# Cross-attention, mixture of experts and self-attention on one core: two hand-written step lists for the first and the steady walk, and the second batch's keys loaded apart from its values

## The reference

```python
x = x + xattn(layernorm(x), ctx)      # softmax((q Wq + bq)(ctx Wk + bk) / 8) (ctx Wv + bv) Wo + bo
z = layernorm(x)
h = z + rmsnorm(causal_attention(z) @ wo)
dense = h + rmsnorm(silu(h @ w1) * (h @ w3) @ w2)
sparse = rmsnorm(sum over the top 2 experts of prob * expert(z))
out = x + dense + sparse
```

## Time and profile before

| | us |
|---|---|
| three runs | 1542.5, 1551.01, 1550.32 |
| median | 1550.32 |
| the profiled execution | 1540.53 (span of its instructions 1538.8) |
| PE busy | 1357.7 (88%) |
| PE weight loads busy | 844.2 |
| DVE, ACT, POOL busy | 812.8, 572.5, 591.5 |
| granted TensorE clock, mean | 0.966 of 2.4 GHz |

### The profile page before, as it was taken

The page is one execution under the profiler, slowest core; times in us unless marked ns, Lnnn a source line. Parts: engine busy times, 40 slices in busy tenths (PEclk is TensorE's granted clock), DMA queues, the critical chain, the costliest instruction groups (busy, mean ns, idle before and its releaser), DMA issues. The chain is left out here.

```text
span 1538.8 us, 21916 instructions
## 1 busy us (share of the span) xinstructions
PE 1357.7 (88%) x6989; PEld 844.2 (55%) x6990; DVE 812.8 (53%) x1656; ACT 572.5 (37%) x1207; POOL 591.5 (38%) x1040
## 2 busy tenths in 40 slices
PE   6997759997999898989979997989899879999995
PEld 5443425663566366646745663566366536666664
DVE  2442554476447626853774486348536823333348
ACT  2334325402630452155125403531452253443446
POOL 4111224324432534254234324331634155555544
PEclk9998969998999999999999999999999999999998
DMA  6128530350043007100700340052005434332245
GB/s 206 48 97 255 202 98 1 92 142 15 1 125 110 15 1 198 43 8 28 206 16 1 110 125 15 1 157 77 15 4 144 128 100 127 127 99 86 89 169 200
DMA packets 82264, 141.61 MB, mean 92 GB/s; under 512 B 10632, under 2 KB 66336, under 8 KB 78720
## 3 DMA queue, kind: packets, MB, share of 16 engines
q1 hardware_dynamic: 62512, 94.37, 20.2%
q10 hardware_dynamic: 13184, 28.34, 6.3%
q0 software_dynamic: 6480, 17.77, 3.4%
HBM read 84.90 MB, written 55.15 MB: 91 GB/s over the span
## 5 line engine op out<-in xcount | busy, mean ns | idle before, releaser
L1325 ACT ACTIVATE room<-ps 128x512 f32<-128x512 f32 x320 | 180.5, 598 | 175.7 <-PE ps L1061 175.0
L1648 DVE TENSOR_REDUCE nm<-ps 128x2 f32<-128x256 f32 (+3 forms) x256 | 200.2, 819 | 82.2 <-PE ps L1035 80.5
L1116 PE MATMUL ps<-hT,w 128*128 128x512 f32 x768 | 207.5, 414 | 0.0
L731 POOL TENSOR_SCALAR_AFFINE_SELECT room<-room 128x256 f32<-128x256 f32 (+1 forms) x320 | 119.8, 384 | 148.7 <-ACT room L1325 146.2
L1116 PEld LDWEIGHTS ps<-hT,w 128*128 128x128 f32 x768 | 141.5, 192 | 34.0 <-DVE hT L1678 2.0
L1034 PE MATMUL ps<-room 96*128 96x128 bf16 (+3 forms) x512 | 125.0, 312 | 32.1 <-DMA room<-parts_d 16.0
L965 PE MATMUL ps<-room,xnT 128*128 128x512 f32 x256 | 131.9, 640 | 20.7 <-ACT xnT L1211 14.5
L1061 PE MATMUL ps<-room 99*128 99x384 bf16 (+3 forms) x512 | 113.0, 310 | 29.5 <-ACT room L1325 26.9
L1152 PE MATMUL ps<-room 128*128 x284 | 135.4, 599 | 1.9 <-ACT room L1375 1.9
L1347 ACT ACTIVATE room<-ps 128x512 f32<-128x512 f32 x64 | 37.2, 592 | 267.5 <-PE ps L1116 267.5
L1126 PE MATMUL ps<-w,room 128*128 128x256 f32 x512 | 129.4, 392 | 8.1 <-DVE room L1699 8.1
(11 more groups left out here) (245 smaller groups left out, 2265.4 us busy)
## 6 DMA issues: line engine op xcount, KB each, us to landing
room<-parts_d SPq DMA_DIRECT2D x48, 256.0 KB, 9.8
room<-parts_d ACTq DMA_DIRECT2D x48, 256.0 KB, 7.4
room<-xs_d SPq DMA_DIRECT2D x71, 129.0 KB, 2.1
parts_d<-room SPq DMA_DIRECT2D x64, 128.0 KB, 1.8
vw_d<-stage ACTq DMA_DIRECT2D x8, 1024.0 KB, 4.4
room<-pair_d SPq DMA_DIRECT2D x8, 1024.0 KB, 8.0
m_d<-stage ACTq DMA_DIRECT2D x8, 896.0 KB, 5.6
room<-m_d SPq DMA_DIRECT2D x7, 1024.0 KB, 5.1
```

What stands on the lines that cost most here:

```text
L731: done(g.affine_select(out=w, in_=w, compare_op=ALU.is_ge, fill=0.0, base=0, pattern=[[0, 2]] * (blocks - 1) + [[1, P]], channel_multiplie ...
L1116: last = mm(bank(up_banks(b, m)[i]), w[:, x, k, m * P:(m + 1) * P], hT[:, y, k, :], start=((x, y, k) == terms[0]), stop=((x, y, k) == term ...
L1325: done(fn(prob[:, u * 512:(u + 1) * 512], bank(score_bank(b) + n % 2), ACT.Exp), "b_exp")
L1648: done(v.tensor_reduce(nm[:, t, 2 * hp:2 * hp + 2], pair_ps, AX.X, ALU.max, negate=True), "a_max")
```

## The change

The dealing functions go, and two lists written out by hand stand in their place, `FIRST_WALK` and `STEPS`, with the same steps as before in them (162 and 205). Counted on the lists:

- In the steady list the part up to `norm_3` is ordered anew. From there to the end it is as it was but for one step: `f_wo_sq` stands behind `qk.0` and `qk.1`, where it stood ahead of them.
- In the first walk nearly everything has another place. The last three `vw_out` stand at the very end, behind `vf.7.1`.
- `kv_in` is split: keys (`m_d`, `bqk_d`) count on it, values (`vw_d`) on a new semaphore `vw_in`. In the first walk SP issues the keys of batch 1 ahead of `send_shifts`; the values stay behind all writes of `vw_d`.
- Of the value folds DVE now copies bank 5, ACT only bank 4; and the projections `vp` go to banks 6 and 7 in turn.
- The copies that turn `wq` and `wk` stand on DVE in step `ct.2.0` of the first walk, not in `qk.0`.

```diff
-STEPS = interleaved() + TAIL
+STEPS = dealt("""
+    x_turn.0 x_turn.1 cs.0.0 f_hb sc.0.0 sc.0.1 cs.0.1 sc.0.2 sc.0.3 sc.0.4 shift.1 sc.0.5 cs.1.0 sc.0.6 sc.0.7 exp.0 va.0.0 sc.0.8 sc.0.9 sum.0
...
+    cv.2.0 cv.2.1 out_t.2 ct.3.0 ct.3.1 va.3.1 va.3.2 cv.3.0 out_t.3 cv.3.1 norm_3 f_o_turn x2_turn.0 f_wo.0 x2_turn.1 f_wo.1 qk.0 qk.1 f_wo_sq
+    f_o_norm qk.2 qk.3 v.0 v.1 f_h_turn v.2 v.3 route.0 fu.0.0 f_yb fg.0.0 fu.0.1 fg.0.1 route.1 fu.1.0 fg.1.0 fu.1.1 fg.1.1 route.2 fd.0.0 fd.0.1
...
+FIRST_WALK = dealt("""
+    x_stats x_apply kp.0 m.0 m.1 kp.1 x_turn.0 x_bias m.2 kf.0.0 x_turn.1 m.3 kf.0.1 cs.0.0 bqk.0 bqk.1 kf.1.0 cs.0.1 kp.2 vw.0 kf.1.1 exp.0 vw.1
...
+    max.6.1 max.6.2 max.6.3 vf.7.0 nx_apply max.7.0 max.7.1 vf.7.1 max.7.2 vw_out.5 vw_out.6 max.7.3 vw_out.7 shift_parts.1 z w_split
...
-            def load_kv(n):
+            def load_keys(n):
                 need(sp, n - 1, "sc_ps", T)
                 need(sp, n - 1, "sc_add", T)
-                need(sp, n - 1, "pv_ps", T)
...
+            def load_values(n):
+                need(sp, n - 1, "pv_ps", T)
...
-                    send_shifts(b, 0)
                     if c is None:
                         for i in range(2):
                             sp.wait_ge(m_out[i], 16 * KD * PAIRS // 4)
                         sp.wait_ge(p0["bqk_out"], 16)
+                        sp.sem_inc(freed, 1)
+                        load_keys(b + 1)
+                    send_shifts(b, 0)
+                    if c is None:
                         for i in range(4):
                             sp.wait_ge(kv_out[i], 16 * PAIRS // 4)
                         sp.sem_inc(freed, 1)
-                        load_kv(b + 1)
+                        load_values(b + 1)
...
-                        for j in range(2):
-                            last = fn(vw_stage[pa % 4][:, half * 2:half * 2 + 2, j * D:(j + 1) * D], bank(4 + j).rearrange("p (c m) -> p c m", m=D), ACT.Copy)
-                        last.then_inc(p0["fold_act"], 1)
+                        fn(vw_stage[pa % 4][:, half * 2:half * 2 + 2, 0:D], bank(4).rearrange("p (c m) -> p c m", m=D), ACT.Copy).then_inc(p0["fold_act"], 1)
...
+                    elif kind == "vf":
+                        pa, half = step[1:]
+                        dve.wait_ge(p0["fold_ps"], 2 * PAIRS + 2 * pa + half + 1)
...
+                        v.tensor_copy(vw_stage[pa % 4][:, half * 2:half * 2 + 2, D:], bank(5).rearrange("p (c m) -> p c m", m=D)).then_inc(p0["fold_dve"], 1)
```

More of the change, by code:

```diff
@@ L51 @@
 PER = dict(
-    x_in=16, kv_in=64, stats=4, stats1=1, mv1=1, rstd1=1, xn1=1, xT1=2, xnT=2, bq=1,
+    x_in=16, kv_in=32, stats=4, stats1=1, mv1=1, rstd1=1, xn1=1, xT1=2, xnT=2, vw_in=32,
     m_ps=10, m_act=8, m_dve=2,
@@ L98, in interleaved @@
-def interleaved():
-    first, last = CROSS.index(("cs", 0, 1)), CROSS.index(("ct", 3, 1))
-    slots = [i for i, s in enumerate(CROSS) if s[0] in ON_PE and first <= i <= last]
-    order, given = [], 0
-    for i, s in enumerate(CROSS):
-        order.append(s)
-        if i in slots:
-            want = (slots.index(i) + 1) * len(SCORES) // len(slots)
-            order += SCORES[given:want]
-            given = want
-    return order
-TAIL = [
[4 rows of a table removed]
-]
-_max = [("max", hp, t) for hp in range(H // 2) for t in range(T)]
@@ L140, in first_walk, with dealt @@
-def first_walk():
-    order = [("x_stats",), ("x_apply",)]
-    cross = [s for s in CROSS_FIRST if not of_previous(s)]
-    tail = [s for s in TAIL if not of_previous(s)]
-    slots = [i for i, s in enumerate(cross) if s[0] in ON_PE and i >= cross.index(("m", 3))]
-    given = 0
-    for i, s in enumerate(cross):
-        order.append(s)
-        if i in slots:
-            want = (slots.index(i) + 1) * len(K_FOLDS) // len(slots)
-            order += K_FOLDS[given:want]
-            given = want
-    given = 0
-    for s in tail:
-        order.append(s)
-        at_max = s[0] == "max" and s[2] % 2 == 1
-        want = given + (3 if s[0] in ("route", "slots") else 1 if s[0] == "v" else 2 if at_max else 0)
-        order += V_FOLDS[given:want]
-        given = min(want, len(V_FOLDS))
-    assert given == len(V_FOLDS), given
-    return order + [("w_split",)]
+def dealt(text):
+    return [(w[0], *map(int, w[1:])) for w in (word.split(".") for word in text.split())]
@@ L164, in steps_of @@
+""")
 def steps_of(attention, net, ahead=True):
     if attention:
-        return [s for s in STEPS if ahead or s[0][:2] != "nx" and s[0] not in ("f_y", "z")] if net else first_walk()
+        return [s for s in STEPS if ahead or s[0][:2] != "nx" and s[0] not in ("f_y", "z")] if net else FIRST_WALK
     first, second = SCORES.index(("va", 0, 1)), SCORES.index(("va", 1, 1))
@@ L981, in batch @@
                         vw = vw_first if c is None else vw_next
+                        if half == 0 and t == 0 and c is not None:
+                            pe.wait_ge(sems["vw_in"], c * per["vw_in"] + per["vw_in"])
                         if half == 0:
@@ L1431, in _ @@
                     done(v.scalar_tensor_tensor(to[rows, which, half * CK:(half + 1) * CK], bank(6 + i % 2, 4 * CK).rearrange("p (a n) -> p a n", a=4)[rows, :, :], scale,
-                                                bias[rows, which].unsqueeze(2).to_broadcast([CHD, 4, CK]), ALU.mult, ALU.add), "kv_in", 8)
+                                                bias[rows, which].unsqueeze(2).to_broadcast([CHD, 4, CK]), ALU.mult, ALU.add), "kv_in", 4)
             n_link = [0]
```

101 lines of the change are left out of this document (53 added, 48 removed), and 8 rows, old and new, of tables (CROSS_FIRST, TAIL).

## The result

The kernel after takes 1505.6 us (median of four, 1501.1 to 1509.5) against 1546.9 us of the kernel before beside it: a ratio of 0.973, 95% interval 0.969 to 0.978. The profiled execution took 1501.1 us with a span (first to last instruction) of 1499.3, 39.5 us less than the span of before. The forecast was 1517 us, within 1494 to 1541.

A forecast was written before the change was run, and what follows sets the result against it. PE was taken to bound the steady cross stage, standing still 7.2 of 64 us. From the profiled 1540.5, -58 (cross stages) + 30 (`f_wo_sq`) - 5 (first walk) gave -33, so the median 1550.3 became 1517 us, range 1494 to 1541.

The forecast's parts named there:

- Steady cross stage: Cross stage of the seven steady walks: score units ahead of `exp.0` on ACT shorten PE's waits, 58 us gained.
- the term of 7.0 us per clean walk: Steady cross stage: an undisturbed walk gains 7.0 us, 1.9 of it from the clock, bounds 5.1 and 8.2.
- my upper bound: Steady cross stage: at most 8.2 us gained per clean walk, if no wait comes beyond those found.
- the 0.9 for waits not found: Steady cross stage: 0.9 us per walk allowed for unfound waits, beside 1.2 us of waits found.
- `f_wo_sq`, the chain: Middle of steady walks: late squares delay `ri`, `f_h_turn` and the loads, 4.3 us a walk, 30 us lost.
- `f_wo_sq`, the clock: Middle of steady walks: clock may fall in the new 3.7 us stop, up to 1.9 us a walk; counted as nothing.
- the rival of 13 us: Clock falls in the new stop of each steady walk, uncovered: 13 us worse, 1530 us; chance 0.15.
- First walk: First walk up to the second walk's first cross score: 206.4 against 211.79, 5 us gained, between 18 gained and 5 lost.
- some 145: Sign in the profile after: the steady walk from `z` to `z` takes some 145 us.
- Hidden delay: Middle of steady walks: the delay of `f_wo_sq` is hidden, 30 us less, priced at 1494 us; chance 0.12.
- Half given back in the cross stage: Steady cross stage: new waits of 3 to 4 us per walk behind `x_bias` or exponentials, 1541 us; chance 0.14.
- Slower: Steady walks: the whole 7.4 us delay of `ri` reaches PE, clock falls twice, 76 us lost, 1563 us; chance 0.05.

The follow-up runs named there:

- exp_ahead: The kernel after with `exp.0` back ahead of `sc.0.2` in the steady list, nothing else: 1543.5 us, 0.998 of before.
- sq_back: The kernel after with `f_wo_sq` put back ahead of `qk.0` in the steady list: 1460.0 us, 0.943 of before.
- sq_between: The kernel after with `f_wo_sq` between `qk.0` and `qk.1`: 1473.2 us, 0.952 of before.
- w13_early: sq_back with w1 and w3 loaded right behind the second batch's keys, and `w_split` waiting for the last `vw_d` writes: 1447.2 us, 0.936 of before.
- end_all: w13_early with `vw_out.3` to `vw_out.7` dealt earlier and `w_split` moved behind `x_turn.1` of the second walk: 1436.3 us, 0.929 of before.
- keys_late: The kernel after with the second batch's keys loaded behind all writes, right ahead of the values: 1507.3 us, 0.975 of before.

## Why the prediction was right, and where it wasn't

- **Total.** -33 was forecast against the profiled execution, -39.5 came. The cross stages gained 70.0 us (58 forecast), the first walk up to the first cross score 9.4 (5), and `f_wo_sq` lost 40.0 in middles and maxima (30). So both gains and the loss were put too small, and a total that is 6.5 us off owes something to luck.
- **Steady cross stage.** The mechanism stood: PE's long wait was an order matter of ACT's queue, exp_ahead brings it back with its price, and no wait came further on; `x_bias` was harmless. Of the waits that I laid out, the score unit waits 0.5 us (0.75 forecast) and `va.0.0` 1.2 us in three of the six later walks (0.3 forecast) and nothing in the other three, where the clock is low at the start of the walk. Mis-sized was the term of 7.0 us per clean walk: the stage takes 58.4 us from `x_turn` and 67.0 before, 8.6, which is above even my upper bound. (That bound, 8.2, should have been 7.9: 7.0 and the 0.9 for waits not found.) The 0.9 was not needed. Beside that, PE's busy time itself fell, from 56.84 to 55.36 us at the same clock of 0.97, for which no term stood; why, no run shows. And the clock, which I had at 1.00, is 0.97 in three of the six, so the 1.9 us from it came only in the other three.
- **`f_wo_sq`, the chain.** Step by step the timeline came out nearly to a tenth in the walk from which it was worked out: squares behind part 2 of `qk.0`, DVE idle until the root, `f_h_turn` 3.1 us later than before relative to the stage's start (3.2 forecast), the first feed-forward matmul 4.6 later (4.4 forecast), the first maximum 4.6 later (4.3 forecast). The mean of seven walks is 5.4, though, and that is the mis-sized term. The middle ends when the loads have landed. They leave 4.6 us later in the mean (4.4 forecast), and from the first issue to the last landing they take 17.2 us instead of 16.3, which I had at nothing. The walk that I costed hides this, since its loads were already slow before (17.2 us, a wait of 2.77 us against 2.3 in the mean). Why they take longer stays open.
- **`f_wo_sq`, the clock.** It fell in the new stop: 0.92 to 0.96 in the middle after, 1.00 before, in sq_back and (0.99 in one) in sq_between. The Trainium skill (TensorE: Matmul & The Clock Gate, Part 1: The HAM clock gate) says that PE's clock is halved after idling, and the trace agrees with it by these numbers. But its price is mostly covered, as I wrote: PE is busy 13.1 us longer in the middles, and still waits 2.2 to 3.5 us for the loads at the end of each. What gets through is 6.4 us in maxima and cross stages against sq_back, and by the estimate at sq_back at most 5 us in the middles. So leaving the clock at nothing was wrong by 6 to 11 us, and the rival of 13 us had the fall right and its place and price wrong: it charged the middles alone.
- **First walk.** First maximum at 135.8 (136 forecast). The maxima took 41 us (45 taken, 37.5 to 50 bounded), and the last fold's copy came at 175.7 (178). The three writes together held SP to 185.0, 9.8 us from their issue (10.5). The estimate from the Trainium skill (DMA: Bandwidth & Descriptors, Bandwidth) was 9.2, and the measurement lies between; the page's figure is for loads that GpSimd issues, and these are writes from ACT. The loads took 12.6 (13.1), PE stood still 23.1 us (24 forecast), and the first cross score came at 202.4 (206.4), so 9.4 us gained instead of 5: of the 4.0 missing, the maxima make 2.8, the writes 0.7 and the loads 0.5. "If the walk were not held by w1 and w3 the earlier maxima would show in full" is shown by w13_early to end_all, where PE's 23 us of standing still go to 0.8. "The keys help only by those 1.5 MB" is shown by keys_late.
- **Signs.** The walk from `z` to `z` takes 146.9 us, not "some 145". That sign did not follow from the prediction's own terms: the maxima of the first walk were to end 20.9 us earlier and the walk only 5, so 16 us of waiting move into the seven, and (1045 - 28 + 16) / 7 is 147.6.
- **Rivals.** Hidden delay: false, 46 us say so. Half given back in the cross stage: false. Slower: it needed 9 us lost a walk; 5.4 in the middle and 0.3 in the maxima came. The range held.

## What to carry to other kernels

When engines read one order, cost a moved step on every engine that has a part in it, and follow the queue behind it: here four squares of 0.4 us, moved by two steps, cost 46 us, because each engine in turn put a wait behind a wait, and unrelated steps stood behind those. A wait's price is not a property of the wait but of what covers it on the waiting engine, so take it again for the new order. Look for what ends a stage: here it was the landing of twelve loads, so a delay counted by how much later they left, and a slower PE ahead of them counted for little. And cost a term on all walks of the trace, not on one: the walk that I took was one of the two with the slowest loads.
